# Moving the B and C convolution taps ahead on VectorE, folding the norm weight into the output weights, and taking y_lo on GpSimd, in a fused Mamba-2 and FFN kernel

## The chip, the cores and the metric

The kernel runs on one core of one Trainium2 chip. The metric is the device time of one execution in microseconds (us), lower is better. Engines are named as the profile names them: PE is TensorE, DVE is VectorE, ACT is ScalarE, POOL is GpSimd, SP is SyncE (it issues the DMAs).

## The reference

Input x is (2, 512, 512): two sequences of 512 tokens, 512 channels. All is fp32.

```
xn   = layernorm(x)
proj = xn @ in_proj_w.T              # gate (8192) | x, B, C (8192 + 1024 + 1024) | dt (128)
xBC  = silu(causal depthwise conv, 4 taps, of the x, B, C columns + bias)
y    = Mamba-2 chunked scan: 8 groups, 128 heads of 64, state 128, chunk 128
       per chunk: (C B^T * exp(cs_l - cs_s), lower triangle) @ (x*dt) + C @ state * exp(cs) ; + x*D
yg   = y * silu(gate)
out  = (yg * rsqrt(mean over the group of yg^2 + eps)) * norm_w  @ out_proj_w.T
ffn  = W2 (silu(W1 xn) * W3 xn), weights 4 bit with scales
x + out * silu(ffn)
```

## The kernel before, in words

Every large product is made with split numbers: an operand is kept as hi (rounded to the matmul's format) and lo (the rest), and the product is hi·hi + lo·hi + hi·lo, three matmuls of 128x512 for each 128 channels (`split_mm`, L125 to L131). The hi part is an ACT copy, the lo part a subtraction on POOL, and for y_lo on DVE.

The main part runs over 16 **bodies**: one per group and sequence (body n has sequence n % 2 and group n // 2). A body has 8 **steps** k = 0 to 7, one for each tile of 128 channels (two heads). Each engine has its own program, written out by hand in the order `step(body, k)`; semaphores alone tie the engines together. The work is software-pipelined, so a step handles several tiles at once. In step k:

- **PE**: C·state of the last tile (L465, out of `c_t`,`state`); the projection of the x tile k+3 into bank `ps_a` (L493); the scores product of tile k (L503); the chunk states (L465, out of `xw`); the gate projection of tile k+2 into bank `ps_g` (L531); the output projection of tile k-2 with `y_hi`,`y_lo` and the output weights (L545 to L547); then extras; then the four transposes of tile k+1 (L585). Extras: in k = 3 and 4 the projection of the next body's B and C into `ps_g` (`project_bc`), in k = 6 the C·B product (`gm`), in k = 7 the transposes of B, in k = 0 the sums of squares of the body before (L562). `ps_g` is one bank, shared by gate, B, C and these, so in k = 4 and 5 the gate projection waits until the DVE taps have read B or C out of it (L524), and what follows a gate projection waits until ACT has copied the gate out (`gev_done`).
- **ACT**: eight Exp of tile k+1 (L712); the hi parts of weights (L681, L686, L691, L701); in k = 4, 5 the first tap of B or C (L737); the first tap of x tile k+3 (L745); y_hi of tile k-1 with the norm weight as scale (L752); its square (L759); in even k the Silu of two gates (L719), of two x tiles (L725) and of B or C (L777); the gate out of `ps_g` (L788), last.
- **DVE**: xdt (L925), xw (L928), ec (L934); in k = 0, 7 the copies of B and C·B; in k = 2 four accumulations of the output (L959) and three small copies of parameters (L915 to L917, to `cw`, `nw`, `dc`); the minimum that bounds the exponent of tile k+2 (L968); the masked product of tile k+1 (L979, `lm` times `gm`); y (L987); the states (L994, L999); in k = 4, 5 the other three taps of B or C; the three taps of x tile k+3 (`taps`, L892); y_lo of tile k-1 (L1015).
- **POOL**: y plus the state part (L1160), times the gate (L1164), the lo parts of weights (L1169, L1174, L1178, L1182), the sum of squares (L1188).

Output weights are converted in the bodies of sequence 0, one tile a step. Before the bodies come a layernorm and the dt chain (to about 88 us), behind them the FFN (from about 1875 us).

Of the kernel before, what the change touches and what calls it, by code (L numbers as in the profile page):

```python
# [143 lines left out]
def build(nc, x, w_conv, w_gate, w_out, w_dt, conv_p, norm_p, head_p, consts, w1q, w1s, w3q, w3s,  # L144
# [9 lines left out]
    with ExitStack() as ctx:  # L154
# [23 lines left out]
        cw = alloc(main, "cw", [2, CONVS, 5])  # L178
# [5 lines left out]
        nw = alloc(main, "nw", [2, TILES])  # L184
        dc = alloc(main, "dc", [2, TILES])
# [100 lines left out]
        whi_x, whi_b, whi_g, whi_o = sem("whi_x"), sem("whi_b"), sem("whi_g"), sem("whi_o")  # L286
        wlo_x, wlo_b, wlo_g, wlo_o = sem("wlo_x"), sem("wlo_b"), sem("wlo_g"), sem("wlo_o")
        par_done = sem("par_done")
# [383 lines left out]
        def _(act):  # L672

            def weights(body, k):

                bd, kx = at(body, k, 4)
                if bd.exists():
                    m = TILES * bd.n + kx
                    act.wait_ge(rawx_in[kx % 2], 16 * (TILES // 2 * bd.n + kx // 2 + 1))
                    wait(act, xp_done, m - 1)  # L680
                    act.activation(conv_hi[kx % 2][:, :, :], raw_x[:, kx % 2, :].rearrange("p (k j) -> p k j", k=KT),  # L681
                                   ACT.Copy).then_inc(whi_x, 1)
                for bd, i in bc_piece(body, k):
# [8 lines left out]
                for group, pos in out_piece(body, k):  # L692
                    act.wait_ge(rawo_in, 16 * (TILES * group + pos + 1))
                    if body.is_number(0) and pos == 0:
                        act.wait_ge(xnt_done, TT)
                    if body.is_number(0) and pos == 4:
                        act.wait_ge(cs_out, 16 * SEQS)
                        act.wait_ge(e_out, 16 * SEQS)
                        act.wait_ge(qt_tr, NQ * SEQS)
                    wait(act, o_done, 2 * TILES * (group - 1) + TILES + pos + 1)  # L700
                    act.activation(wout_hi[pos // 4][:, pos % 4, :], raw_o[:, :], ACT.Copy).then_inc(whi_o, 1)  # L701
# [24 lines left out]

            def work_b(body, k):
                n = TILES * body.n + k
                nx = body.plus(1)
                if k in (4, 5) and nx.exists():  # L730
                    i = k - 4
                    act.wait_ge(bp_done, 2 * nx.n + i + 1)
                    wait(act, bs_done, 2 * nx.n + i)
                    if i == 0:
                        act.wait_ge(par_done, 3 * (nx.n + 1))
                    pos = BC_POS[i]
                    act.activation(z[:, 2, :], ps_g[:, :], ACT.Identity, scale=cw[:, nx.seq, pos, 3:4],  # L737
                                   bias=cw[:, nx.seq, pos, 4:5]).then_inc(tap0_b, 1)
                bd, kx = at(body, k, 3)
                if bd.exists():  # L740
# [4 lines left out]
                    act.activation(z[:, kx % 2, :], ps_a[:, :], ACT.Identity, scale=cw[:, bd.seq, pos, 3:4],  # L745
                                   bias=cw[:, bd.seq, pos, 4:5]).then_inc(tap0_x, 1)
# [15 lines left out]
                if k % 2 == 0:  # L762
# [19 lines left out]

                bd, kg = at(body, k, 2)
                if bd.exists():
                    m = TILES * bd.n + kg
                    act.wait_ge(gate_done, m + 1)
                    wait(act, yg_done, m - 3)
                    act.activation(gate[:, kg % 4, :], ps_g[:, :], ACT.Copy).then_inc(gev_done, 1)  # L788
# [95 lines left out]
        def _(dve):  # L884

            def taps(bd, pos, zi, src, ready, done, i):

                dve.wait_ge(ready, i + 1)
                for d in range(1, 4):
                    if d > 1:  # L890
                        dve.wait_ge(done, 3 * i + d - 1)
                    dve.scalar_tensor_tensor(z[:, zi, d:SEQ], src[:, 0:SEQ - d], cw[:, bd.seq, pos, 3 - d:4 - d],  # L892
                                             z[:, zi, d:SEQ], ALU.mult, ALU.add).then_inc(done, 1)

            def step(body, k):
# [11 lines left out]
                if k == 2 and nx.exists():  # L907
                    if nx.is_number(0):
                        dve.wait_ge(small_in, 16 * 5)
                        dve.wait_ge(dc_done, 2)  # L910
                    wait(dve, tap0_x, TILES * (nx.n - 1))
                    wait(dve, taps_b, 6 * (nx.n - 1))
                    wait(dve, taps_x, 3 * TILES * (nx.n - 1))
                    wait(dve, lo_done, TILES * (nx.n - 1))
# [35 lines left out]

                if k == 2 and before.exists():
# [20 lines left out]
                bd, k1 = at(body, k, 1)  # L972
                if bd.exists():
                    m = TILES * bd.n + k1
                    dve.wait_ge(exp_done, m + 1)
                    if k1 == 0:
                        dve.wait_ge(gm_done, bd.n + 1)
                    lm_c = lm[m % 3][:, :, :].rearrange("p (j c) l -> p j (c l)", j=2)
                    dve.tensor_tensor(lm_c, lm_c, gm[:, :, :].rearrange("p c l -> p (c l)").unsqueeze(1)  # L979
                                      .broadcast_to((P, 2, SEQ)), ALU.mult).then_inc(sc_done, 1)  # L980

                if body.exists():
# [3 lines left out]
                    dve.wait_ge(par_done, 3 * (body.n + 1))  # L986
                    dve.scalar_tensor_tensor(yt[:, k % 2, :], xt[:, k % 4, :], dc[:, body.seq, k:k + 1], ps_y[:, :],  # L987
# [18 lines left out]
                if k in (4, 5) and nx.exists():  # L1006
# [129 lines left out]
        def _(pool):  # L1136
# [12 lines left out]
            def step(body, k):  # L1149
# [34 lines left out]
                if pv.exists() and kp > 0:  # L1184
# [3 lines left out]
                    pool.tensor_tensor(sq_sum[:, :], sq_sum[:, :], sq[:, :], ALU.add).then_inc(sqa_done, 1)  # L1188
                if k == 3 and body.is_number(0):
# [128 lines left out]
```

## Time and profile before

| what | value |
|---|---|
| median of 3 runs | 2064.63 us (2064.29 to 2065.51) |
| the profiled execution: its time | 2066.06 us |
| the profiled execution: its span, first to last instruction | 2064.3 us |
| mean granted TensorE clock | 0.961 of full |
| busy: PE, DVE, ACT, POOL | 1858.4, 1528.2, 1208.6, 1129.5 us |
| HBM traffic | 98 GB/s over the span |

Busy time is the union of an engine's instructions; idle time before an instruction is put down to what released it. Step times are read off PE: from the end of one step's transposes (L585) to the end of the next step's.

### The profile page before, as it was taken

What the parts mean: (1) busy time and instruction counts of PE and PEld (TensorE: products, weight loads), DVE (VectorE), ACT (ScalarE), POOL (GpSimd) and SP (SyncE); (2) the same over time, 40 slices, a digit from 0 to 9 for tenths busy, and PEclk for the clock granted to TensorE, in tenths of its full rate; (3) what the DMA queues carried; (4) which work ended last, traced back from release to release, by engine and by line L of the source; (5) the groups of instructions that cost most, each with busy time, mean ns of one, the idle gap of its engine ahead of it and who ended that gap; (6) DMA issues with size and microseconds to landing.
All of it is one profiled execution on the core that took longest, in us unless ns stands there. A gap on an engine that the chain in (4) does not pass through costs nothing.

```text
span 2064.3 us, 30313 instructions
## 1 busy us (share of the span) xinstructions
PE 1858.4 (90%) x10292; PEld 1504.8 (73%) x10292; DVE 1528.2 (74%) x2363; ACT 1208.6 (59%) x2394; POOL 1129.5 (55%) x746
## 2 busy tenths in 40 slices
PE   4799999898989999998989898999999898998998
PEld 3677777676767777776767676777777676777777
DVE  5567868686877778786868687777868696886850
ACT  3775657565756666565756566665656565752320
POOL 2365646464655556554745466555645475554651
PEclk9899999999999999999999999999999999999999
DMA  3532323232422233232323232232323232233522
GB/s 104 165 103 91 96 89 115 73 103 75 123 91 92 81 110 108 68 106 80 127 83 99 75 113 95 81 102 92 115 79 105 73 121 77 93 116 93 144 90 96
DMA packets 122995, 203.48 MB, mean 99 GB/s; under 512 B 23328, under 2 KB 60576, under 8 KB 122592
## 3 DMA queue, kind: packets, MB, share of 16 engines
q1 hardware_dynamic: 121984, 198.47, 30.2%
q10 hardware_dynamic: 864, 3.15, 0.4%
q8 instruction: 81, 1.33, 0.3%
q14 instruction: 66, 0.54, 0.1%
HBM read 194.23 MB, written 7.34 MB: 98 GB/s over the span
## 4 chain that ended last, share of the span: by engine, by line
PE 49%; DVE 29%; issue 10%; ACT 6%; POOL 4%; DMA 1%; DVEq 0%; SPq 0%; ACTq 0%; POOLq 0%
PE bank L128 9%; PE bank L130 8%; PE bank L129 8%; DVE z L892 7%; DVE lm L979 5%; PE bank L465 4%; PE bank L545 4%; PE bank L546 4%; PE bank L547 4%; DVE lm L968 3%; DVE state L999 3%; PE bank L667 3%; PE bank L503 2%; PE bank L585 2%; DVE yt L987 2%
## 5 line engine op out<-in xcount | busy, mean ns | idle before, releaser
L1160 POOL TENSOR_TENSOR yt<-yt,ec 128x384 f32<-128x384 f32 x128 | 203.5, 1590 | 678.6 <-DVE ec L934 678.6
L892 DVE SCALAR_TENSOR_TENSOR z<-bank,cw,z 128x511 f32<-128x511 f32 (+2 forms) x480 | 355.7, 746 | 11.8 <-ACT z L745 0.5
L128 PE MATMUL bank<-xn_hi,gate_hi 128*128 128x512 f32 x512 | 233.9, 457 | 111.6 <-DVE z L892 111.6
L925 DVE TENSOR_TENSOR xdt<-bank,hp 128x512 f32<-128x512 f32 x128 | 88.3, 690 | 325.5 <-PE bank L585 325.5
L712 ACT ACTIVATE lm<-lm,hp 128x128 f32<-128x128 f32 x1024 | 313.0, 389 | 0.8
L979 DVE TENSOR_TENSOR lm<-lm,gm 128x1024 f32<-128x1024 f32 x128 | 264.5, 2066 | 38.8 <-ACT lm L712 38.8
L128 PE MATMUL bank<-xn_hi,conv_hi 128*128 128x512 f32 x640 | 263.3, 411 | 31.1 <-DVE z L892 31.1
L130 PE MATMUL bank<-xn_hi,conv_lo 128*128 128x512 f32 x640 | 251.9, 394 | 0.0
L129 PE MATMUL bank<-xn_lo,conv_hi 128*128 128x512 f32 x640 | 251.2, 393 | 0.0
L1164 POOL TENSOR_TENSOR yt<-yt,gate 128x512 f32<-128x512 f32 x128 | 237.6, 1856 | 18.4
L1169 POOL TENSOR_TENSOR conv_lo<-raw_x,conv_hi 128x512 fp32r<-128x512 f32 x128 | 210.6, 1646 | 44.9 <-ACT conv_hi L681 44.9
L745 ACT ACTIVATE z<-bank,cw 128x512 f32<-128x512 f32 x128 | 99.1, 774 | 213.9 <-PE bank L130 213.9
L129 PE MATMUL bank<-xn_lo,gate_hi 128*128 128x512 f32 x512 | 223.1, 436 | 0.0
L130 PE MATMUL bank<-xn_hi,gate_lo 128*128 128x512 f32 x512 | 222.6, 435 | 0.0
L128 PEld LDWEIGHTS bank<-xn_hi,gate_hi 128*128 128x128 f32 x512 | 107.4, 210 | 137.7 <-issue 89.2
L545 PE MATMUL bank<-wout_hi,y_hi 128*128 128x512 f32 x512 | 203.9, 398 | 0.0
L546 PE MATMUL bank<-wout_lo,y_hi 128*128 128x512 f32 x512 | 202.6, 396 | 0.0
L547 PE MATMUL bank<-wout_hi,y_lo 128*128 128x512 f32 x512 | 200.7, 392 | 0.0
L968 DVE SCALAR_TENSOR_TENSOR lm<-hp,lm 128x1024 f32<-128x1024 f32 x128 | 185.6, 1450 | 5.1 <-DMA hp<-hp_d 5.1
L788 ACT ACTIVATE gate<-bank 128x512 f32<-128x512 f32 x128 | 75.5, 590 | 177.0 <-PE bank L130 175.3
L752 ACT ACTIVATE y_hi<-yt,nw 128x512 fp32r<-128x512 f32 x128 | 92.4, 722 | 142.1 <-POOL yt L1164 142.1
L128 PEld LDWEIGHTS bank<-xn_hi,conv_hi 128*128 128x128 f32 x640 | 121.6, 190 | 56.1 <-issue 23.2
(130 smaller groups left out, 4063.9 us busy)
## 6 DMA issues: line engine op xcount, KB each, us to landing
lm<-cs_d SPq DMA_DIRECT2D x128, 512.0 KB, 3.9
raw_x<-w_conv_dram SPq DMA_DIRECT2D x128, 256.0 KB, 3.0
ec<-e_d SPq DMA_DIRECT2D x256, 96.0 KB, 3.6
raw_g<-w_gate_dram SPq DMA_DIRECT2D x64, 256.0 KB, 2.7
raw_o<-w_out_dram SPq DMA_DIRECT2D x64, 256.0 KB, 2.7
raw_b<-w_conv_dram SPq DMA_DIRECT2D x32, 256.0 KB, 3.2
q_raw<-w1q_dram SPq DMA_DIRECT2D x10, 256.0 KB, 3.3
q_s<-w1s_dram SPq DMA_DIRECT2D x10, 256.0 KB, 3.5
```

Of the source, the lines that this page charges most:

```text
L128: pe.matmul(dst, a_hi, b_hi, start=(i == 0), stop=False)
L129: pe.matmul(dst, a_hi, b_lo, start=False, stop=False)
L130: mm = pe.matmul(dst, a_lo, b_hi, start=False, stop=(i == len(terms) - 1))
L545: pe.matmul(ps_o[c][:, :], y_hi[:, ko % 2, o], w[0], start=first, stop=False)
L546: pe.matmul(ps_o[c][:, :], y_hi[:, ko % 2, o], w[1], start=False, stop=False)
L547: mm = pe.matmul(ps_o[c][:, :], y_lo[:, ko % 2, o], w[0], start=False, stop=last)
L712: e = act.activation(lm[m % 3][:, u, :], lm[m % 3][:, u, :], ACT.Exp, bias=hp[bd.seq][:, Q_CS, k1, u:u + 1])
L892: dve.scalar_tensor_tensor(z[:, zi, d:SEQ], src[:, 0:SEQ - d], cw[:, bd.seq, pos, 3 - d:4 - d], z[:, zi, d:SEQ], ALU.mult, ALU.add).then_i ...
L968: dve.scalar_tensor_tensor(lm[m % 3][:, :, :], hp[bd.seq][:, Q_CS, kr, :].unsqueeze(2).broadcast_to((P, 2 * NC, CHUNK)), -1.0, lm[m % 3][: ...
L979: dve.tensor_tensor(lm_c, lm_c, gm[:, :, :].rearrange("p c l -> p (c l)").unsqueeze(1) .broadcast_to((P, 2, SEQ)), ALU.mult).then_inc(sc_d ...
L1164: pool.tensor_tensor(yt[:, kp % 2, :], yt[:, kp % 2, :], gate[:, kp % 4, :], ALU.mult).then_inc(yg_done, 1)
L1169: pool.tensor_tensor(conv_lo[kx % 2][:, :, :], raw_x[:, kx % 2, :].rearrange("p (k j) -> p k j", k=KT), conv_hi[kx % 2][:, :, :].bitcast(F ...
```

## The change

1. The taps of B and C: on ACT the first tap moves from `work_b` into `weights`, behind the x weights' hi part and ahead of the other weights; on DVE the other three taps move from behind the states to just behind ec (and ahead of the minimum).
2. In the steps called crowded (k = 2 with a body before, k = 4 and 5 with a body behind) the masked product moves on DVE from behind the minimum to the end of the step, behind the x taps. It is also written as scalar_tensor_tensor (times 1.0, times gm) in place of tensor_tensor, in every step.
3. The norm weight no longer scales y_hi and y_lo; ACT scales the raw output weights in place (64 new activations, with a wait of ACT on itself), then converts them. y_lo becomes a plain subtraction and goes from DVE to POOL, behind the sum of squares.
4. The per-body copies of `cw`, `nw`, `dc` go away; the taps and y read the full tables.
5. On ACT the gate's copy out of `ps_g` moves in even steps ahead of the Silu of B or C and of the second x tile.

```diff
@@ ACT: weights
+                nx = body.plus(1)
+                if k in (4, 5) and nx.exists():
+                    i = k - 4
+                    act.wait_ge(bp_done, 2 * nx.n + i + 1)
+                    wait(act, bs_done, 2 * nx.n + i)
...
+                    act.activation(z[:, 2, :], ps_g[:, :], ACT.Identity, scale=cw_all[:, nx.group, pos, 3:4],
+                                   bias=cw_all[:, nx.group, pos, 4:5]).then_inc(tap0_b, 1)
...
+                    act.activation(raw_o[:, :], raw_o[:, :], ACT.Copy, scale=nw_all[:, group, pos:pos + 1]
+                                   ).then_inc(ws_o, 1)
+                    act.wait_ge(ws_o, TILES * group + pos + 1)
                     act.activation(wout_hi[pos // 4][:, pos % 4, :], raw_o[:, :], ACT.Copy).then_inc(whi_o, 1)
@@ ACT: work_b
-                    act.activation(y_hi[:, kp % 2, :], yt[:, kp % 2, :], ACT.Copy, scale=nw[:, pv.seq, kp:kp + 1]
-                                   ).then_inc(hi_done, 1)
+                    act.activation(y_hi[:, kp % 2, :], yt[:, kp % 2, :], ACT.Copy).then_inc(hi_done, 1)
...
-                if k % 2 == 0:
+                if k % 2 == 1:
+                    gate_raw(body, k)
+                else:
...
+                    gate_raw(body, k)
                     if k in (4, 6) and nx.exists():
@@ DVE
-                    dve.tensor_copy(cw[:, nx.seq, :, :], cw_all[:, nx.group, :, :]).then_inc(par_done, 1)
-                    dve.tensor_copy(nw[:, nx.seq, :], nw_all[:, nx.group, :]).then_inc(par_done, 1)
-                    dve.tensor_copy(dc[:, nx.seq, :], dc_all[:, nx.group, :]).then_inc(par_done, 1)
...
+                if k in (4, 5) and nx.exists():
+                    taps(nx, BC_POS[k - 4], 2, ps_g, tap0_b, taps_b, 2 * nx.n + k - 4)
+
                 if k == 2 and before.exists():
...
-                    dve.tensor_tensor(lm_c, lm_c, gm[:, :, :].rearrange("p c l -> p (c l)").unsqueeze(1)
-                                      .broadcast_to((P, 2, SEQ)), ALU.mult).then_inc(sc_done, 1)
+                crowded = (k == 2 and before.exists()) or (k in (4, 5) and nx.exists())
+                if not crowded:
+                    scores(body, k)
...
-                if k in (4, 5) and nx.exists():
-                    taps(nx, BC_POS[k - 4], 2, ps_g, tap0_b, taps_b, 2 * nx.n + k - 4)
                 bd, kx = at(body, k, 3)
                 if bd.exists():
                     taps(bd, X_POS[kx], kx % 2, ps_a, tap0_x, taps_x, TILES * bd.n + kx)
-
-                if pv.exists():
-                    dve.wait_ge(hi_done, n)
-                    wait(dve, o_done, n - 2)
-                    dve.scalar_tensor_tensor(y_lo[:, kp % 2, :], yt[:, kp % 2, :], nw[:, pv.seq, kp:kp + 1],
-                                             y_hi[:, kp % 2, :].bitcast(F32), ALU.mult, ALU.subtract).then_inc(lo_done, 1)
+                if crowded:
+                    scores(body, k)
@@ DVE: scores(body, k), new
+                    dve.scalar_tensor_tensor(lm_c, lm_c, 1.0, gm[:, :, :].rearrange("p c l -> p (c l)").unsqueeze(1)
+                                             .broadcast_to((P, 2, SEQ)), ALU.mult, ALU.mult).then_inc(sc_done, 1)
@@ POOL, behind the sum of squares
+                if pv.exists():
+                    pool.wait_ge(hi_done, n)
+                    wait(pool, o_done, n - 2)
+                    pool.tensor_tensor(y_lo[:, kp % 2, :], yt[:, kp % 2, :], y_hi[:, kp % 2, :].bitcast(F32),
+                                       ALU.subtract).then_inc(lo_done, 1)
```

## Rows read from the trace of the kernel before

**Rows 1.** The page's busy time of each engine, whole span.
```profile
PE 1858.4 (90%) x10292; PEld 1504.8 (73%) x10292; DVE 1528.2 (74%) x2363; ACT 1208.6 (59%) x2394; POOL 1129.5 (55%) x746
```

**Rows 2.** Busy time by window: body 0, then bodies 1 to 14.
```profile
core 0: us, PE busy (x) PEld busy (x) DVE busy (x) ACT busy (x) POOL busy (x), PEclk, DMA share, GB/s
87.56:196.66 109.10, 99.01 (x552) 79.91 (x553) 79.97 (x130) 71.75 (x146) 65.71 (x41) 0.93 0.31 103
196.66:1773.65 1576.99, 1440.81 (x8236) 1168.69 (x8235) 1220.01 (x1905) 992.15 (x1988) 907.47 (x588) 0.96 0.30 95
```

**Rows 3.** PE's groups in bodies 1 to 14: busy, mean ns, idle before.
```profile
L128 PE MATMUL bank<-xn_hi,conv_hi 128*128 128x512 f32 x560 | 228.6, 408 | 13.0 <-DVE z L892 13.0
...
L128 PE MATMUL bank<-xn_hi,gate_hi 128*128 128x512 f32 x448 | 205.4, 459 | 104.1 <-DVE z L892 104.1
```

**Rows 4.** PE's other waits in bodies 1 to 14: total, times, longest.
```profile
PE bank L465 <- ACT gate L788: 12.1, 14, 0.9
PE bank L562 <- ACT gate L788: 6.9, 14, 0.5
```

**Rows 5.** Busy time by window: the steps k = 0 to 7 of body 8.
```profile
985.46:998.37 12.91, 12.41 (x78) 10.08 (x78) 11.51 (x17) 8.58 (x13) 9.31 (x7) 1.00 0.30 106
998.37:1009.67 11.30, 11.30 (x71) 9.26 (x70) 10.27 (x18) 8.79 (x24) 8.58 (x6) 1.00 0.34 115
1009.67:1021.05 11.38, 11.38 (x71) 9.19 (x70) 11.23 (x17) 6.41 (x10) 9.25 (x6) 1.00 0.32 105
1021.05:1036.29 15.24, 14.31 (x82) 11.58 (x82) 11.12 (x18) 11.49 (x27) 7.96 (x5) 1.00 0.43 137
1036.29:1055.82 19.53, 15.81 (x82) 12.76 (x82) 11.52 (x18) 13.38 (x25) 8.93 (x6) 0.91 0.22 65
1055.82:1072.60 16.78, 13.06 (x70) 10.49 (x70) 11.51 (x18) 5.78 (x15) 7.67 (x5) 0.90 0.24 74
1072.60:1085.93 13.33, 12.46 (x79) 10.13 (x78) 10.03 (x15) 8.70 (x15) 7.79 (x5) 1.00 0.30 95
1085.93:1097.65 11.72, 11.72 (x75) 9.70 (x74) 10.64 (x16) 8.64 (x23) 7.84 (x5) 1.00 0.27 85
```

**Rows 6.** Busy time by window: step 5 of body 7, step 4 of body 0.
```profile
942.78:960.40 17.62, 13.90 (x70) 11.10 (x70) 11.52 (x18) 5.57 (x14) 7.67 (x5) 0.81 0.22 71
132.97:153.71 20.74, 17.02 (x82) 13.63 (x82) 11.51 (x18) 13.37 (x25) 8.92 (x6) 0.84 0.21 61
```

**Rows 7.** Timeline of PE, step 4 of body 8: start, us, instruction, idle before.
```profile
1040.66 0.94 PE L465 MATMUL bank<-xw,b_tok 128*128 128x128 f32 x6
1045.32 0.47 PE L128 MATMUL bank<-xn_hi,gate_hi 128*128 128x512 f32 x1 [3.72 <-DVE z L892]
```

**Rows 8.** Timeline of DVE in the same step.
```profile
1037.40 0.55 DVE L934 TENSOR_TENSOR ec<-bank,ec 128x384 f32<-128x384 f32 x1
1037.87 1.21 DVE L968 SCALAR_TENSOR_TENSOR lm<-hp,lm 128x1024 f32<-128x1024 f32 x1
1039.00 2.03 DVE L979 TENSOR_TENSOR lm<-lm,gm 128x1024 f32<-128x1024 f32 x1
...
1042.86 4.53 DVE L892 SCALAR_TENSOR_TENSOR z<-bank,cw,z 128x511 f32<-128x511 f32 x6
```

**Rows 9.** Timeline of ACT in the same step: the first tap of B.
```profile
1037.01 0.76 ACT L737 ACTIVATE z<-bank,cw 128x512 f32<-128x512 f32 x1
```

**Rows 10.** Single lines, whole span: duration ns min/median/max.
```profile
L968 DVE SCALAR_TENSOR_TENSOR lm<-hp,lm x128: 1211/1215/2291, 68.1 to 1834.5; 128x1024 f32<-128x1024 f32 x128
L979 DVE TENSOR_TENSOR lm<-lm,gm x128: 1218/2036/2322, 83.8 to 1846.2; 128x1024 f32<-128x1024 f32 x128
L1015 DVE SCALAR_TENSOR_TENSOR y_lo<-yt,nw,y_hi x128: 739/743/1455, 107.8 to 1866.4; 128x512 fp32r<-128x512 f32 x128
L1188 POOL TENSOR_TENSOR sq_sum<-sq_sum,sq x112: 1262/1292/2110, 119.0 to 1867.0; 128x512 f32<-128x512 f32 x112
L752 ACT ACTIVATE y_hi<-yt,nw x128: 707/723/730, 104.7 to 1865.6; 128x512 fp32r<-128x512 f32 x128
```

More of the change, by code:

```diff
@@ L682, in weights @@
                                    ACT.Copy).then_inc(whi_x, 1)
+                nx = body.plus(1)
[3 more added lines that the diff above has]
+                    wait(act, bs_done, 2 * nx.n + i)
+                    if i == 0 and nx.is_number(0):
+                        act.wait_ge(small_in, 16 * 5)
+                    pos = BC_POS[i]
+                    act.activation(z[:, 2, :], ps_g[:, :], ACT.Identity, scale=cw_all[:, nx.group, pos, 3:4],
+                                   bias=cw_all[:, nx.group, pos, 4:5]).then_inc(tap0_b, 1)
                 for bd, i in bc_piece(body, k):
@@ L700, in weights @@
                     wait(act, o_done, 2 * TILES * (group - 1) + TILES + pos + 1)
+                    if body.is_number(0) and pos == 0:
+                        act.wait_ge(small_in, 16 * 5)
+                    act.activation(raw_o[:, :], raw_o[:, :], ACT.Copy, scale=nw_all[:, group, pos:pos + 1]
+                                   ).then_inc(ws_o, 1)
+                    act.wait_ge(ws_o, TILES * group + pos + 1)
                     act.activation(wout_hi[pos // 4][:, pos % 4, :], raw_o[:, :], ACT.Copy).then_inc(whi_o, 1)
@@ L725, in silu_x, with gate_raw @@
                 act.activation(xt[:, kx % 4, :], z[:, kx % 2, :], ACT.Silu).then_inc(xs_done, 1)
+            def gate_raw(body, k):
+                bd, kg = at(body, k, 2)
+                if bd.exists():
+                    m = TILES * bd.n + kg
+                    act.wait_ge(gate_done, m + 1)
+                    wait(act, yg_done, m - 3)
+                    act.activation(gate[:, kg % 4, :], ps_g[:, :], ACT.Copy).then_inc(gev_done, 1)
             def work_b(body, k):
@@ L729, in work_b @@
                 nx = body.plus(1)
-                if k in (4, 5) and nx.exists():
[L731 to L738, printed above, removed]
                 bd, kx = at(body, k, 3)
@@ L744, in work_b @@
                     wait(act, xs_done, m - 1)
-                    act.activation(z[:, kx % 2, :], ps_a[:, :], ACT.Identity, scale=cw[:, bd.seq, pos, 3:4],
-                                   bias=cw[:, bd.seq, pos, 4:5]).then_inc(tap0_x, 1)
+                    act.activation(z[:, kx % 2, :], ps_a[:, :], ACT.Identity, scale=cw_all[:, bd.group, pos, 3:4],
+                                   bias=cw_all[:, bd.group, pos, 4:5]).then_inc(tap0_x, 1)
                 pv, kp = at(body, k, -1)
@@ L781, in work_b @@
                         silu_x(bd, kx)
[L783 to L788, printed above, removed]
             def step(body, k):
@@ L891, in taps, with scores @@
                         dve.wait_ge(done, 3 * i + d - 1)
-                    dve.scalar_tensor_tensor(z[:, zi, d:SEQ], src[:, 0:SEQ - d], cw[:, bd.seq, pos, 3 - d:4 - d],
+                    dve.scalar_tensor_tensor(z[:, zi, d:SEQ], src[:, 0:SEQ - d], cw_all[:, bd.group, pos, 3 - d:4 - d],
                                              z[:, zi, d:SEQ], ALU.mult, ALU.add).then_inc(done, 1)
+            def scores(body, k):
+                bd, k1 = at(body, k, 1)
+                if bd.exists():
+                    m = TILES * bd.n + k1
+                    dve.wait_ge(exp_done, m + 1)
+                    if k1 == 0:
+                        dve.wait_ge(gm_done, bd.n + 1)
+                    lm_c = lm[m % 3][:, :, :].rearrange("p (j c) l -> p j (c l)", j=2)
+                    dve.scalar_tensor_tensor(lm_c, lm_c, 1.0, gm[:, :, :].rearrange("p c l -> p (c l)").unsqueeze(1)
+                                             .broadcast_to((P, 2, SEQ)), ALU.mult, ALU.mult).then_inc(sc_done, 1)
             def step(body, k):
@@ L905, in step @@
                     dve.tensor_scalar(rstd_sum[:, :], sums(before)[:, 0:NC], EPS, None, ALU.add).then_inc(rs_done, 1)
[L907 to L914, printed above, removed]
-                    dve.tensor_copy(cw[:, nx.seq, :, :], cw_all[:, nx.group, :, :]).then_inc(par_done, 1)
-                    dve.tensor_copy(nw[:, nx.seq, :], nw_all[:, nx.group, :]).then_inc(par_done, 1)
-                    dve.tensor_copy(dc[:, nx.seq, :], dc_all[:, nx.group, :]).then_inc(par_done, 1)
+                if k == 2 and nx.is_number(0):
+                    dve.wait_ge(small_in, 16 * 5)
+                    dve.wait_ge(dc_done, 2)
                 if body.exists():
@@ L985, in step @@
                     wait(dve, sq_done, n - 1)
-                    dve.wait_ge(par_done, 3 * (body.n + 1))
-                    dve.scalar_tensor_tensor(yt[:, k % 2, :], xt[:, k % 4, :], dc[:, body.seq, k:k + 1], ps_y[:, :],
+                    dve.scalar_tensor_tensor(yt[:, k % 2, :], xt[:, k % 4, :], dc_all[:, body.group, k:k + 1], ps_y[:, :],
                                              ALU.mult, ALU.add).then_inc(y1_done, 1)
```

13 lines of the change are left out of this document (1 added, 12 removed).

## The prediction, made before the changed kernel ran

> **What bounds the kernel now.** I read the page's busy times first. PE is busy 90% of the span and the next, DVE, 74% [rows 1]; the reader is to see that PE has little to lose, and to ask where its last tenth goes. The windows say where: in bodies 1 to 14 PE is idle 1576.99 - 1440.81 = 136.18 us, in body 0 109.10 - 99.01 = 10.09 us, and the granted clock is below full in both [rows 2]. Third, PE's groups with their idle time: of the 136.2 us, 104.1 us stand ahead of the gate projection and 13.0 us ahead of the x projection, both ended by DVE's taps [rows 3], and 12.1 and 6.9 us are waits for ACT's copy of the gate out of `ps_g` [rows 4]. That is all of it (136.1). So a third engine, a DMA or the loads of weights end no wait of PE here.
>
> Last, the steps of one body. Six of the eight take 11.30 to 15.24 us and PE works nearly through them; steps 4 and 5 take 19.53 and 16.78 [rows 5]. The timeline of step 4 shows why: PE is through with the chunk states at 1041.60 and starts the gate projection at 1045.32, 3.72 us later [rows 7], since the taps of B come behind ec, minimum, masked product, y and states on DVE [rows 8]. ACT had the first tap ready at 1037.77 [rows 9], before DVE was through with ec.
>
> The stall costs a second time. Steps 3 and 4 hold the same PE work (gate, x, output and one B or C projection), yet PE is busy 14.31 us in the one and 15.81 in the other, at a granted clock of 1.00 and 0.91; step 5 holds that of step 2, 11.38 us, and takes 13.06 at 0.90 [rows 5], in the body before 13.90 at 0.81 [rows 6]. The clock is full (2.4 GHz) in the steps whose waits are below 1 us and falls in part to the half level (1.2 GHz) in the two steps with a wait of 3.72. So a body pays 1.50 + (1.68 + 2.52)/2 = 3.60 us for the low clock, which I expect to go with the stall.
>
> **The change, part by part.** *B and C taps early.* 28 gate projections wait in bodies 1 to 14, 104.1 us, and the clock adds 14 x 3.60 = 50.4 us. After the change DVE is through with ec 1.66 us behind the step's start (1037.95 against 1036.29) [rows 5, 8]. ACT's first tap needs only the projection that PE ends ahead of the transposes, and takes 0.76 us [rows 9]. Three taps take 4.53 / 2 = 2.27 us [rows 8], so `ps_g` is read out at 3.9 us, and PE asks for it at 1041.60 - 1036.29 = 5.3 us [rows 7]: 1.4 us to spare. The whole stall goes: -104.1 and -50.4 us. What is late next: the minimum and y move back by the 2.27 us, forward by the masked product (2.03 us [rows 8]) that is now last; the x taps are due only at the next x projection, behind the transposes, and they come no later than now.
>
> *Masked product last in step 2.* There the x taps are late by 0.93 us (13.0 us in 14 bodies [rows 3]); the masked product ahead of them takes 1.22 to 2.32 us [rows 10], so the wait goes: -13.0 us. The product is due at the next step's score product, behind an x projection of 12 matmuls (about 3 us), so its being last costs nothing; without that cover it would cost its own 2 us a step.
>
> *scalar_tensor_tensor for tensor_tensor.* The trace has both at 128x1024: the minimum 1.21 us at best, the masked product 1.22 us at best, and both rise to 2.3 us [rows 10] where they meet a POOL instruction. I take no difference: 0 us. The ends are -0.8 us (the medians, 2.04 against 1.22) and +0.3 us each, and neither is on PE's path.
>
> *y_lo on POOL.* DVE loses 0.74 to 1.46 us a step. POOL gains one 128x512 instruction like the sum of squares, 1.29 us (1.26 to 2.11) [rows 10]. POOL's busiest step is 9.31 us [rows 5]; with it 10.6 us, at worst 11.4, against 11.3 us of PE at least. PE needs y_lo at the output projection of the next step, 5.3 us plus a gate projection (12 matmuls, some 3 us) into it. Hidden by PE: 0 us; if POOL's step passed 11.3 us, each us above would cost one in every short step. Here a page of the Trainium skill speaks against the change: "Perfetto Trace Analysis", section "Optimizing Scalar/DVE Operations", says that GpSimd and VectorE share an SBUF read port, so that moving work between them might not help. "GPSIMD Engine Reference", section "Engine selection", puts two-input work at about twice VectorE's time, by which y_lo would take about 1.5 us. The masked product of step 4 does show such a meeting (2.03 us for 1.22) [rows 8, 10]. By the rule the freed time on DVE is paid back in waits between the two; that is rival 1.
>
> *Norm weight into the weights.* 64 more activations with a scale, at the 0.72 us of L752 [rows 10], between nothing and 1 us with the wait on itself, in sequence 0 bodies alone: ACT is busy there 5.8 to 13.4 us a step [rows 5], the large one being step 4, which has 4 us of stall in it to give. 0 us on the path; y_hi loses its scale, which I also count as nothing. The three copies that go were hidden behind PE: 0.
>
> *Gate copy ahead of the Silus.* It serves the waits of rows 4. In step 6 PE waits for the copy and then for C's Silu, which now follows it, so one activation (about 0.5 us) of the 0.87 is won; in step 0 the sum of squares on POOL is nearly as late. I take 12.1 + 6.9 down to about 7: -12 us.
>
> **Sum.** Bodies 1 to 14: 104.1 + 13.0 + 12.0 + 50.4 = 179.5 us. Body 0: idle 10.09 less 0.7 that stays, and clock 17.02 - 14.31 = 2.7 in step 4 and about 2.5 in step 5 [rows 5, 6]: 14.6 us. Body 15 has no B or C behind it; its step 2 wait and half its step 0 wait: 1.2 us. Together 195.3. I give 3 us back for new waits of tenths that I can't see: 192. From the profiled span, 2064.3 - 192 = 1872; its own time lies 1.8 us above its span, and the median of the runs 1.4 us below that time, so 1872.
>
> **Checks of the floor.** PE's work in a body at full clock is 12.41 + 11.30 + 11.38 + 14.31 + 14.31 + 11.38 + 12.46 + 11.72 = 99.3 us [rows 5]. DVE's busy time in the same steps is 87.8 us before y_lo leaves, so about 80 after; ACT's 71.8 + 8 x 0.8; POOL's 67.3 + 8 x 1.3 = 77.7. PE remains the bound with a fifth to spare, and no step alone puts another engine above it by more than the buffers carry over.
>
> **Rivals.** (1) *DVE and POOL get in each other's way.* If both two-input DVE instructions of a step wait for one more POOL instruction each (2 x 1.3 us) and y_lo's 0.74 is gone, DVE gains 1.9 us a step, up to 13.4 in steps of 11.3 to 11.7 us. About 1 us a step would show on PE: 8 x 15 = 120 us given back, 1990 us. Against it: most meetings exist today, and DVE has slack at the next long step. (2) *Half a stall remains.* If ACT reaches the first tap late (it now stands behind Exp, table load and x weights), by 1.4 us plus 1.9, the gate waits 1.9 us twice a body, and the clock may fall again: (3.7 + 3.6) x 15 = 110 us back, 1980 us; with the clock held, 1928. For it: in odd steps the Exps come behind a table load; against it, they are done before the step starts. (3) *GpSimd becomes the bound*: slower than before. Its place is the end of each POOL step, y_lo and what waits behind. It decides from a POOL step of 112.6 / 8 = 14.1 us on; from 9.31 that is 4.8 us for y_lo. At 5.5 us, 14.8 a step, the time would be 2064 + 16 x 8 x 0.7 = 2154 us. Nothing in the rows reaches this; the longest like instruction took 2.11 us. (4) *Nothing moves*, because what is behind the taps in PE's order waits for something else just as late: about 2060. PE's own groups name no such thing.
>
> **How the numbers follow.** My forecast has 0.76, between 1856 (no wait at all left and the clock full: 203 us less, some us for the fill) and 1900 (2 us of new waits a body). Rivals 1 and 2 together have 0.20, spread from 1900 to 1990; rival 4 0.02, rival 3 0.02. The range goes from 1856 to 1920, and so leaves out about 2 in 10. Below 0.2%, or 4 us, a measurement of this kernel can't tell a change from none. Faster 0.96, within it 0.02, slower 0.02.
>
> **What would show it.** Right: in the new profile the idle time ahead of the gate projection is gone, step 4 takes about 14.3 us and step 5 about 11.4, the granted clock is full from body 0 to the last one (mean clock near 0.99), the B taps start right behind ec, a body takes 99.5 to 100.5 us. Wrong: idle time ahead of the score product (xdt or the masked product late: rival 1) or still ahead of the gate projection, ended by the taps (rival 2), or ahead of the output projection, ended by POOL (rival 3). The prediction fails most easily on the clock: if it falls at waits shorter than those I see today, 3.6 us a body come back, or if the masked product in its new form is longer than 2.3 us.

## The result, and the profile after

The changed kernel takes 1855.03 us (median of 4 runs, 1854.23 to 1857.10) against 2064.53 us: a ratio of 0.8986, 95% interval 0.8970 to 0.9002, 209.5 us less. Predicted were 1872 us, in a range from 1856 to 1920. The direction held, and so did the cause named for the large loss, but the time lies 1 us below the range, since the gain was put too low by 17 us. The repeat further down gave 1856.6 us.

The page of the changed kernel, busy time of each engine (compare [rows 1]):

```profile
span 1853.2 us, 30173 instructions
PE 1789.4 (97%) x10292; PEld 1461.7 (79%) x10292; DVE 1419.8 (77%) x2187; ACT 1239.0 (67%) x2458; POOL 1272.3 (69%) x874
```

Busy time by window: body 0, bodies 1 to 14 (as in [rows 2]), then the steps k = 0 to 7 of body 8 (as in [rows 5]). The columns are the window, its length, busy time of PE, PEld, DVE, ACT and POOL, the granted clock and DMA:

```profile
84.28:180.93 96.65, 94.60 (x553) 76.66 (x553) 75.67 (x120) 76.72 (x155) 74.30 (x48) 0.97 0.36 116
180.93:1566.29 1385.36, 1378.77 (x8235) 1130.08 (x8234) 1126.34 (x1750) 1018.80 (x2044) 1027.72 (x700) 1.00 0.34 108
...
873.40:886.04 12.64, 12.37 (x79) 10.08 (x78) 10.14 (x16) 9.43 (x15) 10.54 (x8) 1.00 0.36 102
886.04:897.33 11.29, 11.29 (x70) 9.26 (x70) 8.69 (x14) 9.22 (x24) 9.84 (x7) 1.00 0.34 116
897.33:908.64 11.31, 11.31 (x70) 9.26 (x70) 11.13 (x18) 8.18 (x14) 9.43 (x7) 1.00 0.41 135
908.64:922.70 14.06, 14.06 (x82) 11.50 (x82) 9.77 (x15) 11.15 (x26) 9.12 (x7) 1.00 0.39 130
922.70:936.77 14.07, 14.07 (x83) 11.51 (x82) 11.02 (x17) 12.65 (x24) 10.55 (x7) 1.00 0.27 90
936.77:948.08 11.31, 11.31 (x70) 9.26 (x70) 11.02 (x17) 7.24 (x17) 8.31 (x6) 1.00 0.32 111
948.08:960.84 12.76, 12.43 (x78) 10.11 (x78) 8.70 (x14) 9.12 (x14) 9.04 (x6) 1.00 0.31 99
960.84:972.60 11.76, 11.76 (x75) 9.70 (x74) 9.98 (x15) 9.58 (x25) 9.11 (x6) 1.00 0.25 84
```

Six of the eight steps now have PE busy from end to end. Steps 4 and 5 went from 19.53 and 16.78 us to 14.07 and 11.31, and the granted clock is 1.00 in every step. A body takes 1385.36 / 14 = 99.0 us, less than the 99.5 to 100.5 that the prediction named as a sign, and steps 4 and 5 less than its 14.3 and 11.4. PE's waits in bodies 1 to 14, all there are (as in [rows 3, 4]):

```profile
PE bank L462 <- ACT c_t L790: 4.7, 14, 0.3
PE bank L559 <- POOL sq_sum L1189: 1.9, 7, 0.3
```

The wait ahead of the gate projection (104.1 us) and of the x projection (13.0 us) are gone; 6.6 of 136.2 us of idle time are left. DVE's timeline of step 4 of body 8 (as in [rows 8]) has the taps of B right behind ec:

```profile
923.81 0.55 DVE L944 TENSOR_TENSOR ec<-bank,ec 128x384 f32<-128x384 f32 x1
924.28 2.31 DVE L898 SCALAR_TENSOR_TENSOR z<-bank,cw_all,z 128x511 f32<-128x511 f32 x3
926.50 1.46 DVE L981 SCALAR_TENSOR_TENSOR lm<-hp,lm 128x1024 f32<-128x1024 f32 x1
...
929.75 2.31 DVE L898 SCALAR_TENSOR_TENSOR z<-bank,cw_all,z 128x511 f32<-128x511 f32 x3
931.98 1.99 DVE L910 SCALAR_TENSOR_TENSOR lm<-lm,gm 128x1024 f32<-128x1024 f32 x1
```

They end at 926.59, 3.9 us into the step, and PE starts the gate projection at 927.77, 5.1 us in, without waiting (compare [rows 7]):

```profile
927.08 0.94 PE L462 MATMUL bank<-xw,b_tok 128*128 128x128 f32 x6
927.77 0.48 PE L128 MATMUL bank<-xn_hi,gate_hi 128*128 128x512 f32 x1
```

Where the 211.1 us of span went, before minus after: bodies 1 to 14 1576.99 - 1385.36 = 191.6; body 0 109.10 - 96.65 = 12.5; what lies ahead of body 0 87.56 - 84.28 = 3.3; body 15 and all behind it 290.65 - 286.91 = 3.7. Which edit shortened the stretch ahead of body 0 was not tried; it took 84.3 us here, 85.0 in the repeat of the same kernel, and 85.2 with the taps alone. In bodies 1 to 14, PE's idle time fell by 129.6 us and its busy time, for the same matmuls, by 1440.81 - 1378.77 = 62.0 us.

### The profile page after: what moved, and what is told of

The parts are those of the page before. It is cut to its first block, busy times and chain, and to the rows that moved or that the text cites. A ratio compares the mean times of both kernels' runs of the same rounds, so it can differ in the third digit from the quotient of the medians.

```text
span 1853.2 us, 30173 instructions
## 1 busy us (share of the span) xinstructions
PE 1789.4 (97%) x10292; PEld 1461.7 (79%) x10292; DVE 1419.8 (77%) x2187; ACT 1239.0 (67%) x2458; POOL 1272.3 (69%) x874
## 4 chain that ended last, share of the span: by engine, by line
PE 76%; POOL 7%; DVE 5%; issue 5%; ACT 5%; DMA 2%; SPq 0%; ACTq 0%; POOLq 0%; DVEq 0%
PE bank L128 13%; PE bank L130 12%; PE bank L129 12%; PE bank L462 10%; PE bank L500 6%; PE bank L542 5%; PE bank L544 5%; PE bank L543 5%; PE bank L582 3%; PE bank L664 3%; POOL yt L1161 2%; POOL yt L1165 2%; DMA q_s<-w3s_dram 1%; ACT L731 1%; POOL up_lo L1208 1%
## 5 line engine op out<-in xcount | busy, mean ns | idle before, releaser
L1161 POOL TENSOR_TENSOR yt<-yt,ec 128x384 f32<-128x384 f32 x128 | 175.5, 1371 | 365.0 <-DVE ec L944 365.0
L898 DVE SCALAR_TENSOR_TENSOR z<-bank,cw_all,z 128x511 f32<-128x511 f32 (+2 forms) x480 | 358.2, 746 | 11.8 <-ACT z L756 0.5
L910 DVE SCALAR_TENSOR_TENSOR lm<-lm,gm 128x1024 f32<-128x1024 f32 x128 | 260.9, 2038 | 11.8 <-ACT lm L724 11.8
L128 PE MATMUL bank<-xn_hi,gate_hi 128*128 128x512 f32 x512 | 212.2, 415 | 0.0
L756 ACT ACTIVATE z<-bank,cw_all 128x512 f32<-128x512 f32 x128 | 98.9, 772 | 162.5 <-PE bank L130 162.5
L130 PE MATMUL bank<-xn_hi,gate_lo 128*128 128x512 f32 x512 | 202.0, 395 | 0.0
L129 PE MATMUL bank<-xn_lo,gate_hi 128*128 128x512 f32 x512 | 201.7, 394 | 0.0
L1193 POOL TENSOR_TENSOR y_lo<-yt,y_hi 128x512 fp32r<-128x512 f32 x128 | 181.5, 1418 | 0.0
L1189 POOL TENSOR_TENSOR sq_sum<-sq_sum,sq 128x512 f32<-128x512 f32 x112 | 146.3, 1306 | 6.3 <-ACT sq L769 6.3
L763 ACT ACTIVATE y_hi<-yt 128x512 fp32r<-128x512 f32 x128 | 80.8, 632 | 100.0 <-POOL yt L1165 100.0
```

The source lines that it names most:

```text
L128: pe.matmul(dst, a_hi, b_hi, start=(i == 0), stop=False)
L129: pe.matmul(dst, a_hi, b_lo, start=False, stop=False)
L130: mm = pe.matmul(dst, a_lo, b_hi, start=False, stop=(i == len(terms) - 1))
L910: dve.scalar_tensor_tensor(lm_c, lm_c, 1.0, gm[:, :, :].rearrange("p c l -> p (c l)").unsqueeze(1) .broadcast_to((P, 2, SEQ)), ALU.mult, A ...
L1161: pool.tensor_tensor(yt[:, kp % 2, P:SEQ], yt[:, kp % 2, P:SEQ], ec[kp % 2][:, :], ALU.add).then_inc(add_done, 1)
```

## The experiments

Times are medians of 4 or 5 runs, ratios are to the kernel before on the same chip with the 95% interval. The experiments ran on three chips, on which the kernel before took 2063.4 to 2064.7 us.

**The taps alone.** The kernel before, with the B and C taps moved on ACT and DVE as in the change:

```diff
@@ ACT weights, behind conv_hi of x
+                if k in (4, 5) and nx.exists():
+                    ... first tap of B or C, as in the change, with the per-body copies `cw`
@@ ACT work_b
-                    ... first tap of B or C
@@ DVE, behind gm and ahead of acc
+                if k in (4, 5) and nx.exists():
+                    taps(nx, BC_POS[k - 4], 2, ps_g, tap0_b, taps_b, 2 * nx.n + k - 4)
@@ DVE, behind the states
-                if k in (4, 5) and nx.exists():
-                    taps(nx, BC_POS[k - 4], 2, ps_g, tap0_b, taps_b, 2 * nx.n + k - 4)
```

> The kernel before with part 1 of the change alone: B and C taps early on ACT and DVE, nothing else. If the stall ahead of the gate projection and the low clock behind it are most of the gain: idle ahead of the gate 0, full clock in the bodies, the waits of step 2 (0.93 us) and for the gate copy (0.87, 0.50) stay, 101 to 102 us a body, about 1893 us (1885 to 1900). If DVE becomes the bound with y_lo and the masked product still on it, steps 4 and 5 stay 1 to 2 us above PE's work and the time is above 1920.

Measured: 1958.6 us, ratio 0.9487 (0.9471 to 0.9503). A miss: the stall ahead of the gate is gone, but only half of the gain came. PE's waits in bodies 1 to 14 of this kernel, then its steps 4, 5 and 6 of body 8:

```profile
PE bank L128 <- ACT gate L789: 27.2, 14, 2.0
PE bank L465 <- ACT gate L789: 23.5, 14, 1.7
PE bank L128 <- DVE z L893: 13.0, 14, 0.9
PE bank L562 <- ACT gate L789: 6.8, 14, 0.5
```

```profile
977.11:994.97 17.86, 15.91 (x83) 12.52 (x82) 12.02 (x18) 12.66 (x24) 9.29 (x6) 0.90 0.22 71
994.97:1006.27 11.30, 11.30 (x70) 9.27 (x70) 11.05 (x17) 6.06 (x15) 8.04 (x5) 1.00 0.32 105
1006.27:1020.42 14.15, 12.51 (x78) 10.14 (x78) 10.90 (x17) 8.94 (x15) 7.77 (x5) 1.00 0.27 94
```

Step 5 is cured (11.30), so the rival as put (DVE full, steps 4 and 5 both long) doesn't fit either. In step 6 the old wait for the copy has grown from 0.87 to 1.7 us. Step 4 has a new wait: the projection of C into `ps_g` waits for ACT to copy the gate out. ACT's and DVE's timelines of that step say why the copy is late:

```profile
985.46 0.61 ACT L778 ACTIVATE b_t<-z 128x512 f32<-128x512 f32 x1
988.75 0.63 ACT L735 ACTIVATE xt<-z 128x512 f32<-128x512 f32 x1 [2.67 <-DVE z L893]
989.29 0.58 ACT L789 ACTIVATE gate<-bank 128x512 f32<-128x512 f32 x1
```

```profile
982.30 2.31 DVE L983 TENSOR_TENSOR lm<-lm,gm 128x1024 f32<-128x1024 f32 x1
...
986.41 2.31 DVE L893 SCALAR_TENSOR_TENSOR z<-bank,cw,z 128x511 f32<-128x511 f32 x3
```

The gate's copy stands on ACT behind the Silu of x tile k+3, which waits for the x taps (to 988.72), which stand on DVE behind the masked product. PE no longer loses time ahead of the gate, so it comes to the next use of `ps_g` sooner than the copy does. It waits 1.95 us and the clock falls again (0.90). Two edits could cut this chain, and the change has both: the masked product behind the x taps, and the gate's copy ahead of that Silu.

**The first of them: the masked product last.** The taps alone, plus `scores` (still tensor_tensor) at the end of steps 2, 4 and 5, behind y_lo, which stays on DVE:

```diff
+                crowded = (k == 2 and before.exists()) or (k in (4, 5) and nx.exists())
+                if not crowded:
+                    scores(body, k)
...
+                if crowded:
+                    scores(body, k)
```

> The kernel before with early B and C taps and the masked product last in steps 2, 4 and 5, still as tensor_tensor, y_lo still on DVE ahead of it, norm weight and gate copy as before. If waits of PE each cost their length plus some 0.2 us for the restart: the 0.93 us of step 2 goes with 0.2 us more, 17 us below the run with the taps alone, about 1876 us. If only the wait's length counts, 14 us below.

Measured: 1872.3 us, 0.9070 (0.9055 to 0.9085). The number expected was nearly right (1876), but it lies 86 us below the taps alone and not 17, since that run came out 66 us above its forecast of 1893. The order of DVE is enough to cut the chain. By the two traces a body is 5.9 us shorter: 3.8 in step 4, 0.8 in step 6, 1.2 in steps 2 and 3.

**The second: the gate's copy ahead.** The taps alone, plus the order of the change on ACT; masked product and y_lo as before:

```diff
-                if k % 2 == 0:
+                if k % 2 == 1:
+                    gate_raw(body, k)
+                else:
...
                         silu_x(bd, kx)
+                    gate_raw(body, k)
```

> The kernel before with early B and C taps and the gate's copy ahead of the Silus, masked product and y_lo as before. If the wait of step 4 in the run with the taps alone came from the gate copy standing behind a Silu that waits for the late x taps, it goes without touching the masked product: only step 2's 0.93 us plus 0.24 stays, 100.2 us a body, 1872 to 1880 us. If DVE is simply too full with the taps early, steps 4 and 6 stay long: above 1900.

Measured: 1925.1 us, 0.9332 (0.9316 to 0.9347). Neither forecast (1872 to 1880, or above 1900 with steps 4 and 6 long) fits as put. Step 4's wait for the copy is gone and the clock stays full, as the first had it, but steps 5 and 6 are long (12.6 and 14.9 us). PE's waits in bodies 1 to 14:

```profile
PE bank L128 <- DVE z L897: 31.1, 42, 0.9
PE bank L465 <- ACT c_t L789: 17.6, 14, 1.3
PE bank L585 <- DVE state L1007: 7.7, 14, 0.6
PE bank L562 <- POOL sq_sum L1194: 1.8, 7, 0.3
```

13.0 of the 31.1 us are the old wait of 0.93 us for the x taps of step 2. With B and C taps early and the rest in its old order, DVE falls behind and PE meets it in steps 5 and 6 at four more places: ahead of the gate projection (0.4 us), of the transposes (0.6), of the x projection (0.9) and, by way of C's Silu, of the C·B product (1.3). So the copy alone doesn't do. The previous run (masked product last, y_lo on DVE too, the copy at its old place) has none of these four waits: the masked product has to give way.

**The same two, taken out of the changed kernel.** Gate's copy last in even steps again:

```diff
-                    gate_raw(body, k)
                     if k in (4, 6) and nx.exists():
...
                         silu_x(bd, kx)
+                    gate_raw(body, k)
```

> The changed kernel with the gate's copy last in even steps again. The x taps come early enough in steps 4 and 6 by the masked product being last, so no wait appears in step 4; the waits for the gate copy come back in step 6 (0.87 us) and step 0 (0.50): about 1.0 us a body, 1869 to 1873 us, as in the run with DVE's order alone (99.97 us a body). If the copy's place guards step 4 too, 1.9 us of wait and the low clock there, 1920 or more.

Measured: 1870.9 us, 0.9064 (0.9049 to 0.9079), as expected: the copy's place is worth 14 to 16 us, in steps 6 and 0 alone.

Masked product ahead of y in step 2 again:

```diff
-                crowded = (k == 2 and before.exists()) or (k in (4, 5) and nx.exists())
+                crowded = k in (4, 5) and nx.exists()
```

> The changed kernel with the masked product ahead of y in step 2 (last in 4 and 5 alone). The x taps are late again by some 0.9 us, and the restart costs 0.24 more: 1.2 us a body, 1870 to 1875 us. If the freed parameter copies and y_lo already gave step 2 its room, no difference: 1855.

Measured: 1875.0 us, 0.9084 (0.9068 to 0.9099), at the upper end of what was expected. Step 2 and 3 together take 26.6 us (11.38 and 15.2) and not 25.4: PE's wait is back, 13.0 us in 14 bodies, and with it 0.24 us a body of busy time.

**The taps late, in the changed kernel.** The DVE taps of B and C behind the states:

```diff
-                if k in (4, 5) and nx.exists():
-                    taps(nx, BC_POS[k - 4], 2, ps_g, tap0_b, taps_b, 2 * nx.n + k - 4)
...  behind the states:
+                if k in (4, 5) and nx.exists():
+                    taps(nx, BC_POS[k - 4], 2, ps_g, tap0_b, taps_b, 2 * nx.n + k - 4)
```

> The changed kernel with the three DVE taps of B and C back behind the states, the masked product still last. y waits for PE's score product at 4.4 us into the step either way, so the stall should stay near 3.5 us and the clock should fall again: about 11 us a body, 2015 to 2030 us. The rival, that the masked product ahead of the taps made half of the stall, gives a stall of 1.7 us and about 1910 to 1950.

Measured: 2036.0 us, 0.9865 (0.9848 to 0.9881), 6 us above the range expected. The stall is back in full, and the masked product ahead of the taps had no part in it. PE's wait, then DVE's timeline of step 4:

```profile
PE bank L128 <- DVE z L898: 104.1, 28, 3.7
```

```profile
1018.90 1.22 DVE L979 SCALAR_TENSOR_TENSOR lm<-hp,lm 128x1024 f32<-128x1024 f32 x1
1021.82 0.75 DVE L991 SCALAR_TENSOR_TENSOR yt<-xt,dc_all,bank 128x512 f32<-128x512 f32 x1 [1.70 <-PE bank L500]
...
1023.90 4.53 DVE L898 SCALAR_TENSOR_TENSOR z<-bank,cw_all,z 128x511 f32<-128x511 f32 x6
```

DVE now waits 1.70 us for PE's score product where the masked product stood before. y, states and taps follow PE, so behind them the taps can't be early, whatever goes ahead. All the other edits together are worth 28 us with the taps late.

**The taps half-way**, between y and the states:

```diff
-                if k in (4, 5) and nx.exists():
-                    taps(nx, BC_POS[k - 4], 2, ps_g, tap0_b, taps_b, 2 * nx.n + k - 4)
...  behind y, ahead of the states:
+                if k in (4, 5) and nx.exists():
+                    taps(nx, BC_POS[k - 4], 2, ps_g, tap0_b, taps_b, 2 * nx.n + k - 4)
```

> The changed kernel with the taps of B and C between y and the states: they end at about 7.4 us into the step, the gate is asked for at 5.3, so a wait of about 2.1 us twice a body. If the clock stays full at such a wait: 2 x (2.1 + 0.2) = 4.6 us a body, about 1925 us. If it falls as it does at 3.7 us, another 3 to 4 us a body: 1970 to 1985.

Measured: 1958.2 us, 0.9488 (0.9473 to 0.9504), between the two forecasts. Steps 3, 4 and 5 of body 8, then steps 4 and 5 of body 4:

```profile
963.14:977.21 14.07, 14.07 (x83) 11.52 (x82) 9.76 (x15) 11.15 (x26) 9.15 (x7) 1.00 0.39 130
977.21:995.37 18.16, 15.85 (x82) 12.76 (x82) 10.39 (x17) 12.93 (x25) 9.38 (x7) 0.91 0.23 70
995.37:1009.22 13.85, 11.55 (x71) 9.34 (x70) 10.09 (x17) 6.99 (x16) 8.17 (x6) 1.00 0.26 91
...
555.02:571.64 16.62, 14.32 (x83) 11.60 (x82) 10.43 (x17) 12.94 (x25) 9.42 (x7) 1.00 0.23 75
571.64:586.94 15.30, 13.00 (x70) 10.44 (x70) 10.08 (x17) 6.99 (x16) 8.13 (x6) 0.89 0.26 83
```

The same wait of 2.3 us stands in steps 4 and 5. In step 4 of body 8 the clock falls and PE is busy 15.85 - 14.07 = 1.78 us longer; in step 5 it stays at 1.00 and PE is still busy 11.55 - 11.31 = 0.24 us longer. In body 4 it is the other way round. (In step 5 of the odd bodies the profile puts the wait, of the same 2.3 us, down to GpSimd's lo part of the gate weights and not to the taps.) Over bodies 1 to 14 the clock falls behind 12 of the 14 waits of step 4 and 4 of the 14 of step 5. So the low clock isn't tied to the length of a wait alone, and a wait costs something at full clock too.

**y_lo back on DVE**, in the changed kernel:

```diff
@@ POOL
...
-                    pool.tensor_tensor(y_lo[:, kp % 2, :], yt[:, kp % 2, :], y_hi[:, kp % 2, :].bitcast(F32),
-                                       ALU.subtract).then_inc(lo_done, 1)
@@ DVE, behind the x taps, ahead of scores where crowded
...
+                    dve.tensor_tensor(y_lo[:, kp % 2, :], yt[:, kp % 2, :], y_hi[:, kp % 2, :].bitcast(F32),
+                                      ALU.subtract).then_inc(lo_done, 1)
```

> The changed kernel with y_lo back on DVE, as a plain subtraction behind the x taps (ahead of the masked product in the crowded steps). PE is the bound and DVE has 15 percent of room: 1854 to 1859 us, no difference that counts. If DVE needed the relief, its steps 2 and 5 (11.3 us of PE work) grow by 0.7 to 1.4 us: 1875 to 1895.

Measured: 1855.5 us, 0.8990 (0.8975 to 0.9005): no difference from the changed kernel.

**The masked product as tensor_tensor**, in the changed kernel:

```diff
-                    dve.scalar_tensor_tensor(lm_c, lm_c, 1.0, gm[:, :, :]... , ALU.mult, ALU.mult)
+                    dve.tensor_tensor(lm_c, lm_c, gm[:, :, :]... , ALU.mult)
```

> The changed kernel with the masked product as tensor_tensor again, places as changed. Both forms take 1.22 us at 128x1024 when nothing is in their way and PE is the bound: no difference, 1854 to 1857 us. If the form with a scalar keeps clear of GpSimd, the mean of the masked product is lower with it by several tenths of a us.

Measured: 1856.2 us, 0.8992 (0.8978 to 0.9006): no difference. Its row, and that of the changed kernel (duration ns min/median/max), are the same too:

```profile
L910 DVE TENSOR_TENSOR lm<-lm,gm x128: 1217/2030/2300, 81.3 to 1636.8; 128x1024 f32<-128x1024 f32 x128
```

```profile
L910 DVE SCALAR_TENSOR_TENSOR lm<-lm,gm x128: 1214/2030/2307, 80.7 to 1635.9; 128x1024 f32<-128x1024 f32 x128
```

**y_lo twice on GpSimd**, in the changed kernel:

```diff
+                    pool.tensor_tensor(y_lo[:, kp % 2, :], yt[:, kp % 2, :], y_hi[:, kp % 2, :].bitcast(F32),
+                                       ALU.subtract).then_inc(twin_done, 1)
+                    pool.wait_ge(twin_done, n)
                     pool.tensor_tensor(y_lo[:, kp % 2, :], ...
```

> The changed kernel with y_lo computed twice on GpSimd in every step, the second over the first. It asks how far GpSimd is from being the bound. Its busiest step has 10.6 us of work and would have 12.0, against steps of PE of 11.3 to 12.8: some waits ahead of the output projection or the sum of squares, 1858 to 1885 us. If GpSimd and VectorE block each other enough to set the pace (rival 1 of the prediction), 1 us or more a step: above 1975.

Measured: 1859.9 us, 0.9018 (0.9005 to 0.9032). Bodies 1 to 14:

```profile
182.92:1568.44 1385.52, 1378.90 (x8235) 1130.07 (x8234) 1126.36 (x1750) 1018.84 (x2044) 1194.19 (x813) 1.00 0.34 108
```

GpSimd is busy 1194 of 1386 us and PE doesn't notice: 1385.52 us against 1385.36. The 3 to 5 us come from body 0 (98.4 us for 96.7) and from body 15 and what lies behind it (289.3 for 286.9).

**Two more moves, and the changed kernel beside it.** From the changed kernel: in even steps ACT does B's or C's Silu, the gate's copy, then the Silu of x tile k+2; GpSimd adds the last sum of squares ahead of the weights' lo parts.

```diff
@@ ACT, even steps
-                        silu_x(bd, kx)          # at(body, k, 2)
-                    gate_raw(body, k)
                     if k in (4, 6) and nx.exists():
...
+                    gate_raw(body, k)
...
+                        silu_x(bd, kx)          # at(body, k, 2)
@@ POOL
+                if pv.exists() and kp == 7:     # behind the lo part of x
...
+                    pool.tensor_tensor(sq_sum[:, :], sq_sum[:, :], sq[:, :], ALU.add).then_inc(sqa_done, 1)
...
-                if pv.exists() and kp > 0:      # at its old place
+                if pv.exists() and 0 < kp < 7:
```

> The changed kernel with two more moves against its last waits: on ACT the gate's copy and C's (B's) Silu ahead of the Silu of x tile k+2, on GpSimd the last sum of squares ahead of the weights' lo parts. Idle of PE in bodies 1 to 14 was 6.6 us and goes, with 0.1 us of restart each: 7 to 8 us less, 1846 to 1849 us. If the x tile's Silu, now later, is late for its transposes instead: no gain.

> The changed kernel unaltered, on the same chip and in the same rounds as the two-move version: 1855 us, a ratio to before of 0.898 to 0.899.

Measured: 1842.2 us, 0.8927 (0.8915 to 0.8939), against 1856.6 us, 0.8996 (0.8983 to 0.9008), for the changed kernel: 14.4 us less, twice what was expected, and the fastest version of the study. Bodies 1 to 14 of it:

```profile
178.95:1552.87 1373.92, 1373.92 (x8234) 1130.85 (x8234) 1126.23 (x1750) 1020.03 (x2044) 1027.00 (x700) 1.00 0.34 109
```

No idle time of PE is left there. Step 6 went from 12.77 to 12.20 us for a wait of 0.34, so 0.23 us more than the wait; step 0, in every other body, from 12.63 to 12.13 for a wait of 0.27. That makes 11.5 us in bodies 1 to 14: the 6.6 us of waits and 21 times 0.23. The other 3 us came in body 0 (1.8) and ahead of it.

## Why the prediction was right, and where it was wrong

**The bound and the stall: right.** The 3.72 us ahead of the gate projection in steps 4 and 5 and the low clock behind it were the large loss, the early taps had the 1.2 us to spare, and PE remains the bound. The idle time that the prediction took off bodies 1 to 14 (129.1 us) went to within 0.5 us (129.6).

**The step that failed: the term for PE's longer busy time.** The prediction took off 50.4 us in bodies 1 to 14 for it, all put down to the low clock; measured are 62.0 (PE's busy time, before less after). It priced each wait at the length that the trace prints, and read what the clock costs from steps 4 and 5 against steps 3 and 2, as if these ran undisturbed. But step 3 had its own wait of 0.93 us, and takes 14.31 us of busy time before and 14.07 after at the same clock of 1.00. Against the undisturbed 14.07 and 11.31, steps 4 and 5 of [rows 5, 6] lost 1.74 and 1.75 to 2.59 us (not 1.50 and 1.68 to 2.52), and step 3, counted as nothing, 0.24. The runs show the same 0.23 to 0.24 us at full clock in four other places: the taps half-way (step 5), the masked product early in step 2, and both waits that the last version removed.

The low clock itself was priced about right. Without 0.24 us for each wait, steps 4 and 5 lost 1.5 and, as the mean of the 14 bodies, 1.9 us to it: 48 us in all, for 50.4. What was put at nothing is the 0.24 us at each wait that went: 28 ahead of the gate projection, 14 ahead of the x projection, 7 in step 0, together 11.8 us, the size of what was missed. Both sums are worked out from the step times.

The timelines show what the 0.24 us is. Unhindered, the gate projection starts at 927.77, 0.25 us ahead of the printed end of the chunk states (927.08 + 0.94 = 928.02). With the wait it started 3.72 us behind that end [rows 7]. So from the start of the chunk states to the start of the gate projection it takes 0.69 us after and 4.66 before, 3.97 us more for a wait printed as 3.72; the first gate matmul itself is no longer (0.47 against 0.48). Matmuls overlap in the trace, and idle time counted from the end of the last one begins that much too late.

**The smaller terms.** What lies ahead of body 0 gave 3.3 us and was put at 0; body 15 and behind gave 3.7 for 1.2; body 0 gave 12.5 for 14.6; and the 3 us given back for new waits had no row behind them. With the 11.6 us of the main term and the 0.5 of idle time this is the whole of 211.1 - 192. The lower end of the range, 203 us and some for the fill, was built from the same terms and was short for the same reason: an end of a range made only of the wait lengths that the trace prints is not a floor.

**B and C taps early, credited with 154.5 us: wrong as an attribution.** Alone they gave 105 us (2064.0 to 1958.6). The sentence on what is late next looked at the x projection alone: the x taps are also due at ACT's Silu, and the gate's copy out of `ps_g`, for which PE waits, stood behind it. This is the second rival's form (a stall that remains) at another place, and the masked product's place, put at 13.0 us, was worth 86 us on top of the taps, 17 of them by its place in step 2. Since the change had that edit too, the sum came out nearly right, and in this it was lucky in part: the prediction did count on the x taps coming no later than before, but not on ACT's copy, and so on PE, depending on them.

**The masked product last in step 2, the gate's copy: right.** 19 us for the first (put at 13.0, with nothing for what a wait costs beyond its printed length) and about 15 for the second (put at 12).

**y_lo on GpSimd, the form of the masked product, the weights' scale: right at nothing.** y_lo takes 1.26 to 2.31 us on GpSimd (median 1.30), for the 1.29 and 1.26 to 2.11 that the prediction went by, and on either engine the kernel takes the same time. The folding of the weight and the dropped parameter copies were not tried alone; but the kernel with early taps and the masked product last (0.9070) and the changed one with the gate's copy last (0.9064) differ by them, y_lo and the form together, and their intervals overlap. Rival 1 didn't come about: in bodies 1 to 14 PE waits nowhere for DVE, and 1.9 us in all for GpSimd (the sum of squares). The Trainium skill's "Perfetto Trace Analysis", section "Optimizing Scalar/DVE Operations", says that such a move might not help. It did not: 1855.5 us with y_lo on DVE, 1855.0 without. The two kernels say that PE waits for DVE with neither, not how much the two engines hold each other up. GpSimd as the bound (rival 3) is ruled out with room: even with y_lo done twice, bodies 1 to 14 take 1385.5 us.

## What to carry to other kernels

When one wait of the bound engine is taken away, follow the shared buffer to its next user, not only the next instruction of the moved kind: here 65 of the 209 us hung on ACT's copy out of the bank that gate, B and C share (steps 4 and 6 of the taps alone against the masked product last), and the two edits of the order that looked small (the masked product's place and the copy's) carried as much as the one that was meant. Compare a step that waits with one that doesn't wait at all, since its neighbours may carry smaller waits of their own; and measure a wait from start to start, not by the idle time that is printed. Try the offloads singly too: y_lo on GpSimd, the instruction's form, the folding of the weight and the dropped copies together bought no time that could be told from none.

## What the runs showed of the hardware

- A wait of TensorE cost its printed length plus 0.20 to 0.25 us at full clock, mostly 0.23 or 0.24 (step 3 before against after; step 5 with the taps half-way; steps 6 and 0 of the last version). Ahead of the gate projection this is the overlap of one matmul's record with the next, 0.25 us.
- The granted clock has two levels in these traces, 1.00 and 0.50 (2.4 and 1.2 GHz). In bodies 1 to 14 it fell to the lower one for a while behind all 28 waits of 3.72 us before, behind all 14 of 1.95 us (step 4, taps alone) and behind 16 of 28 of 2.3 us (taps half-way), but behind none of the 14 of 1.7 us (step 6, taps alone). Each fall cost 1.4 to 2.8 us of PE's time beyond the 0.24.
- The price changes for the same wait of 3.72 us. Before, it was 1.5 us in step 4 of bodies 1 to 14 (in body 0 2.7), and in step 5 by turns 1.5 and 2.4. With the taps late in the changed kernel, step 4 had 2.6 to 2.8 in eight bodies and about 1.5 in six. What decides this stays open.
- tensor_tensor and scalar_tensor_tensor at 128x1024 with both inputs in SBUF meet GpSimd in the same way, and what counts is who is running first. With no GpSimd instruction running when it started, the minimum of the kernel before took 1.21 to 1.23 us in all 82 cases, in 80 of which one began while it ran; with one running, it took 1.66 to 2.29 us in all 46. The masked product started with one running in 125 of 128 cases of the changed kernel, and has a median of 2.03 us in either form.
